# Third layer's edges of a graph network: cross product before the first map, destination rows gathered with adding transfers

## The reference, cut to what matters

```python
msg_s = (s_n @ Ws_src)[src] + (s_n @ Ws_dst)[dst]
msg_v = (v_n . Wv_src)[src] + (v_n . Wv_dst)[dst]
y0, y1 = rsh[:, 0], rsh[:, 1:4]
w1 = rbf @ W_rbf                                  # 16 -> 224 numbers an edge
m1_s, m1_v = cg_tp(msg_s, msg_v, y0, y1, *w1)
a = leaky_0.2(m1_s @ W_alpha); a = sum over 16 of (a * alpha_dot)     # 4 logits
val_s, val_v = m1_s @ Ws_val, m1_v . Wv_val
val_v = val_v * sigmoid(val_s @ Wg); val_s = sigmoid(val_s)
m2_s, m2_v = cg_tp(val_s, val_v, y0, y1, fixed weights)
h = m2_s @ Ws_vlin, m2_v . Wv_vlin

def cg_tp(s, v, y0, y1, w_ss, w_sv, w_vs, w_vv0, w_vv1):
    scalars = [w_ss * s * y0, w_vv0 * dot(v, y1) / sqrt(3)]
    vectors = [w_sv * s * y1, w_vs * v * y0, w_vv1 * cross(v, y1) / sqrt(2)]
```

## Time and profile before

| | us |
|---|---|
| median of 3 runs (lowest, highest) | 12669.28 (12666.13, 12681.18) |
| the profiled execution | 12702.04 |
| its span, first to last instruction | 12700.3 |
| mean granted TensorE clock | 0.791 of full speed |
| tables and their barrier | from 75.3 to about 166 |
| second layer's edge phase | from about 4188 to about 6750 |
| third layer's edge phase | from 7285.7 to about 9820 |

### The profile page before, as it was taken

One profiled execution on the slowest core, in us unless ns is written; L12 is line 12 of the kernel. 1 busy time (PEld: TensorE's weight loads), 2 busy tenths in 40 slices (PEclk: granted clock), 3 DMA queues, 4 the chain that ended last, 5 costly groups with the idle time before them and its releaser, 6 DMA issues. The chain is left out here.

```text
span 12700.3 us, 220425 instructions
## 1 busy us (share of the span) xinstructions
PE 9229.7 (73%) x44798; PEld 7244.6 (57%) x44798; DVE 8713.2 (69%) x21701; ACT 4529.6 (36%) x11637; POOL 8172.7 (64%) x8692
## 2 busy tenths in 40 slices
PE   2899999973655666666664578888887465999985
PEld 2888888863545322222223477777776454565654
DVE  4677777777643555555554389999999764667763
ACT  1455555540012222222221267777776001333331
POOL 4788888864843788888882176666664582666650
PEclk7777777776865777777776589999898786899995
...
GB/s 91 106 114 115 113 113 114 115 85 112 170 74 15 111 131 131 131 130 131 130 132 141 102 79 81 81 81 81 81 81 67 129 170 59 84 87 87 93 87 41
DMA packets 1339110, 1293.91 MB, mean 102 GB/s; under 512 B 504078, under 2 KB 1142018, under 8 KB 1338374
## 3 DMA queue, kind: packets, MB, share of 16 engines
...
...
## 5 line engine op out<-in xcount | busy, mean ns | idle before, releaser
L664 POOL DMA_INDIRECT e_gs<-tab_src,e_ix x1568 | 1708.1, 1089 | 763.2 <-issue 429.9
L664 POOL DMA_INDIRECT e_gd<-tab_dst,e_ix x1568 | 1610.7, 1027 | 477.8 <-issue 474.4
L715 PE MATMUL e_psS<-e_rows,e_same 128*128 128x480 f32 x1568 | 1113.6, 876 | 848.2 <-DVE e_same L689 848.2
L603 PE MATMUL e_psF<-w_ident,e_F 128*128 128x128 f32 x6272 | 1293.0, 315 | 246.9 <-ACT e_F L1822 233.0
L733 POOL DMA_INDIRECT acc<-e_sums,e_row x784 | 1247.5, 1591 | 239.0 <-issue 206.7
L715 PEld LDWEIGHTS e_psS<-e_rows,e_same 128*128 128x128 f32 x1568 | 430.6, 293 | 1541.7 <-issue 1514.7
L1642 POOL DMA_INDIRECT e_g<-tab_src,e_er x976 | 970.1, 994 | 525.1 <-issue 284.1
L633 ACT ACTIVATE e_FT<-e_psF 128x384 f32<-128x384 f32 (+1 forms) x2352 | 1078.0, 458 | 538.5 <-PE e_psF L603 526.4
L1431 PE MATMUL s_psS<-s_wv,s_hot 128*128 128x168 f32 (+1 forms) x3904 | 800.0, 361 | 615.2 <-POOL s_wv L1389 242.6
L603 PEld LDWEIGHTS e_psF<-w_ident,e_F 128*128 128x128 f32 x6272 | 895.5, 170 | 389.9 <-issue 346.0
L1431 PEld LDWEIGHTS s_psS<-s_wv,s_hot 128*128 128x128 f32 x3904 | 694.3, 228 | 720.4 <-issue 529.5
...
## 6 DMA issues: line engine op xcount, KB each, us to landing
s_val<-val SPq DMA_DIRECT2D x488, 320.0 KB
val<-e_O SPq DMA_DIRECT2D x392, 320.0 KB, 2.7
acc<-w_zeros SPq DMA_DIRECT2D x392, 139.5 KB
...
e_krow<-in_src_t SPq DMA_DIRECT2D x196, 256.0 KB
...
e_es<-in_es SPq DMA_DIRECT2D x196, 130.0 KB
e_gs<-tab_src,e_ix POOLq DMA_INDIRECT x1568
```

Of the source, the lines that this page charges most:

```text
L603: last = nc.tensor.transpose(psF[:, P * g:P * g + P], F[:, k, P * g:P * g + P], ident[:, :])
L664: pool.indirect_dma_start(into[t][u][:, k, :], None, tables[t], bass.IndirectOffsetOnAxis(ix[u][:, t, k:k + 1], 0))\
L715: nc.tensor.matmul(psS[(k) % len(psS)], T["same"][u][:, k, :], values[:, k, :], start=True, stop=True)\
```

## The change

Four things change, all for the third layer's edges.

1. **Adding transfers.** POOL gathers source rows into `msg` (four buffers), and one step later, when they have landed, gathers destination rows onto them with `compute_op=ALU.add` (line 1931 of the changed kernel). DVE's add of line 1945 and the buffers `gs` and `gd` are gone. POOL's wait for the reuse of a buffer is on `products` of the macro four before.
2. **Cross product first.** DVE makes all nine products of the message's vector with y1 (`nine`, 3 x 96 columns a tile), takes the dot product and the cross product from them, and multiplies the weights in. The map then gives only the part that goes with scalars as a third group of 32, so that after it two DVE instructions (2069, 2075) stand where eight stood. `O` is 292 wide, not 384.
3. **y0 through the weights.** `edge_tables` makes `es16_y0`, the 16 radial rows times y0, once: PE and ACT turn y0, SP stores it as `y0_t`, and then in eight rounds SP loads 8 pieces of `es16` and 8 of y0 (broadcast to 16 partitions), POOL multiplies 128 x 1568, and SP stores 8 pieces. In the edge phase the weight map takes 32 rows (16 plain, 16 scaled), SP loads one more piece a macro, and ACT's four scalings a macro of line 1822 (`e_msg_y`) are gone.
4. **Logits.** The part of the leaky unit that is linear is folded into the map (four columns, 160 to 163), so DVE has max and multiply in one instruction, a sum, and an add of 16 numbers. Setup has a few more small loads and DVE instructions on weights.

The diff, without unchanged lines:

```diff
@@ -394,12 +401,23 @@
+        Q, CH = ET // 7, EPAD // 8
+        PART = CH // 8
+        psY, y0T = S.ps("psY", [Q, 2, 512]), S.sb("y0T", [Q, 7, P])
+        es2, y2 = ([S.sb(f"{name}{u}", [P, PART]) for u in range(2)] for name in ("es2", "y2"))
+        def scaled_out(sp, n):
+            u = n % 2
+            sp.wait_ge(sem("scaled"), n + 1)
+            for c in range(8):
+                at = bass.ds(CH * c + PART * n, PART)
+                sp.dma_start(D["es16_y0"][:, at], es2[u][16 * c:16 * c + 16, :]).then_inc(sem(f"scaled_out{u}"), 16)
@@ -409,10 +427,30 @@
+            y0_row = D["y0_t"].rearrange("t p -> (t p)")
+            for n in range(8):
+                u = n % 2
+                if n > 1:
+                    sp.wait_ge(sem(f"scaled_out{u}"), 128 * (n // 2))
+                for c in range(8):
+                    at = bass.ds(CH * c + PART * n, PART)
+                    sp.dma_start(es2[u][16 * c:16 * c + 16, :], D["es16"][:, at]).then_inc(sem(f"scaled_in{u}"), 16)
+                if n == 0:
+                    sp.wait_ge(sem("y0_T"), 2)
+                    sp.dma_start(D["y0_t"].rearrange("(g q) p -> q g p", q=Q), y0T[:, :, :]).then_inc(sem("y0_out"), 16)
+                    sp.wait_ge(sem("y0_out"), 16)
+                for c in range(8):
+                    at = bass.ds(CH * c + PART * n, PART)
+                    sp.dma_start(y2[u][16 * c:16 * c + 16, :], y0_row[at].partition_broadcast(16)).then_inc(sem(f"scaled_in{u}"), 16)
+                if n:
+                    scaled_out(sp, n - 1)
+            scaled_out(sp, 7)
+            for u in range(2):
+                sp.wait_ge(sem(f"scaled_out{u}"), 128 * 4)
@@ -425,6 +463,10 @@
+            for n in range(8):
+                u = n % 2
+                pool.wait_ge(sem(f"scaled_in{u}"), 256 * (n // 2 + 1))
+                nc.gpsimd.tensor_tensor(es2[u][:, :], es2[u][:, :], y2[u][:, :], ALU.mult).then_inc(sem("scaled"), 1)
@@ -433,6 +475,10 @@
+            for n in range(2):
+                act.wait_ge(sem("y0_turned"), n + 1)
+                a, b = 4 * n, min(4 * n + 4, 7)
+                nc.scalar.activation(y0T[:, a:b, :], psY[:, n, 0:P * (b - a)].rearrange("q (g p) -> q g p", p=P), ACT.Copy).then_inc(sem("y0_T"), 1)
@@ -585,6 +645,49 @@
+X_A, X_D, X_C, X_X, X_B, X_W = 0, 64, 128, 224, 320, 384
+NINE_W, MSG_W = 384, CX + C1V
+def spread(ap, *dims):
+    return bass.AP(ap.tensor, ap.offset, [list(ap.ap[0]), *[list(d) for d in dims]])
+def dve_message_products(nc, dve, i, psW, msg, nine, dot, F, Y, S, free):
+    tt = nc.vector.tensor_tensor
+    v, crossed = msg[:, :, C0:CX], msg[:, :, CX:MSG_W]
+    tt(comp(nine[:, :, 0:3 * C1V]), bcast(v, 2, 3), bcast(Y, 3, C1V), ALU.mult).then_inc(S.sem("nine"), 1)
+    dve.wait_ge(S.sem("nine"), i + 1)
+    nc.vector.tensor_reduce(dot[:, :, :], nine[:, :, :].rearrange("p t (d c) -> p t c d", d=3)[:, :, 0:C1, :], AX.X, ALU.add)\
+        .then_inc(S.sem("dot"), 1)
+    tt(crossed[:, :, 0:C1], nine[:, :, 224:256], nine[:, :, 160:192], ALU.subtract)
+    tt(comp(crossed[:, :, C1:C1V], 2), comp(nine[:, :, 64:128], 2), comp(nine[:, :, 32:352], 2)[:, :, ::-1, 0:C1], ALU.subtract)\
+        .then_inc(S.sem("crossed"), 1)
+    dve.wait_ge(S.sem("weights"), i + 1)
+    wait(dve, *free)
+    tt(spread(F[:, :, X_A:], (X_W, TM), (X_B - X_A, 2), (1, C0)), comp(psW[:, :, 0:2 * C0], 2), bcast(msg[:, :, 0:C0], 2, 2), ALU.mult)
+    dve.wait_ge(S.sem("crossed"), i + 1)
+    tt(comp(F[:, :, X_C:X_C + C1V]), bcast(psW[:, :, 128:160], 2, 3), comp(v), ALU.mult)
+    tt(comp(F[:, :, X_X:X_X + C1V]), bcast(psW[:, :, 192:224], 2, 3), comp(crossed), ALU.mult)
+    dve.wait_ge(S.sem("dot"), i + 1)
+    tt(F[:, :, X_D:X_D + C1], psW[:, :, 160:192], dot[:, :, :], ALU.mult).then_inc(S.sem("products"), 1)
+def pe_message_maps(nc, pe, i, k, FT, o, W, w, rows, S, tag, ahead):
+    scalars = W[w + "_t0"].shape[1]
+    f = FT[:, k, :]
+    wait_apart(pe, S.sem(tag + "_FT"), i * TM + k + 1, S.sem("pe_passed"))
+    wait_apart(pe, S.sem(tag + "_O"), i * TM + k + 1 - ahead, S.sem("pe_passed"))
+    nc.tensor.matmul(o[:, 0:scalars], f[0:rows, 0:P], W[w + "_t0"][:, :], start=True, stop=True, skip_group_check=True)
+    nc.tensor.matmul(o[:, scalars:scalars + P], f[:, P:2 * P], W[w + "_t1"][:, :], start=True, stop=False, skip_group_check=True)
+    nc.tensor.matmul(o[:, scalars + C1:scalars + P], f[:, 2 * P:3 * P], W[w + "_t2"][:, :], start=False, stop=True,
+                     skip_group_check=True).then_inc(S.sem(tag + "_linear"), 1)
@@ -1789,11 +1893,16 @@
+                if m := i_of_ring(0):
+                    i, u, j = m
+                    wait_apart(sp, sem(f"msg{u}"), j * 16 * TM, sem("sp_passed"))
+                    for n, k in enumerate(("src", "dst")):
+                        sp.dma_start(ix[u][:, n, :], D[k][:, bass.ds(i * TM, TM)]).then_inc(sem(f"ix{u}"), 16)
-                    sp_indices(sp, i, u, j, ix, D, ("src", "dst"), S, [sem("gathered0"), sem("gathered1")])
-                    sp.dma_start(es[u][:, :], D["es16"][:, bass.ds(i * ME, ME)]).then_inc(sem(f"es{u}"), 16)
+                    sp.dma_start(es[u][0:16, :], D["es16"][:, bass.ds(i * ME, ME)]).then_inc(sem(f"es{u}"), 16)
+                    sp.dma_start(es[u][16:32, :], D["es16_y0"][:, bass.ds(i * ME, ME)]).then_inc(sem(f"es{u}"), 16)
@@ -1805,11 +1914,22 @@
+            passed = sem("pool_passed")
-                i_of = by_two(i_of_ring)
-                if m := i_of(0):
-                    pool_gather(nc, pool, *m, ix, (D["tab_src"], D["tab_dst"]), (gs, gd), S, (sem("msg"), m[0] - 1))
+                if m := i_of_ring(0):
+                    i, u, j = m
+                    wait_apart(pool, sem(f"ix{u}"), (j + 1) * 32, passed)
+                    wait_apart(pool, sem("products"), i - RING + 1, passed)
+                    for k in range(TM):
+                        pool.indirect_dma_start(msg[u][:, k, 0:CX], None, D["tab_src"], bass.IndirectOffsetOnAxis(ix[u][:, 0, k:k + 1], 0))\
+                            .then_inc(sem(f"from_src{u}"), 16)
+                if m := i_of_ring(ADD):
+                    i, u, j = m
+                    wait_apart(pool, sem(f"from_src{u}"), (j + 1) * 16 * TM, passed)
+                    for k in range(TM):
+                        pool.indirect_dma_start(msg[u][:, k, 0:CX], None, D["tab_dst"], bass.IndirectOffsetOnAxis(ix[u][:, 1, k:k + 1], 0),
+                                                compute_op=ALU.add).then_inc(sem(f"msg{u}"), 16)
@@ -1858,13 +1978,6 @@
-                if m := i_of(JOIN):
-                    i, u, j = m
-                    act.wait_ge(sem("msg"), i + 1)
-                    wait(act, sem("products"), i)
-                    for k in range(TM):
-                        last = times_y0(msg0, msg, i, k)
-                    last.then_inc(sem("msg_y0"), 1)
@@ -1876,9 +1989,9 @@
-                    if m := i_of(JOIN):
+                    if m := i_of(WEIGHTS):
-                        wait_apart(pe, sem(f"es{u}"), (j + 1) * 16, passed)
+                        wait_apart(pe, sem(f"es{u}"), (j + 1) * 32, passed)
@@ -1918,17 +2031,16 @@
-                nc.vector.memset(f[:, :, 352:F_W], 0.0).then_inc(sem("padded"), 1)
+                nc.vector.memset(f[:, :, 96:128], 0.0).then_inc(sem("padded"), 1)
-                    wait(dve, sem("dot"), i)
-                    wait(dve, sem("products2"), i - SECOND_IN + PRODUCT)
-                    dve_products(nc, dve, i, psW, msg, msg0, prod, dot, F[u], Y(i)(0, 3), S,
-                                 (sem("msg"), i + 1), (sem("lin_turned"), (i - 1) * TM), (sem("msg_y0"), i + 1))
+                    _, v, turn = i_of_ring(PRODUCT)
+                    dve.wait_ge(sem(f"msg{v}"), (turn + 1) * 16 * TM)
+                    dve_message_products(nc, dve, i, psW, msg[v], nine, dot, F[u], Y3(i), S, (sem("lin_turned"), (i - 1) * TM))
@@ -1936,33 +2048,31 @@
-                    tt(V2, comp(O[i_of_ring(SECOND_IN)[1]][:, :, 160:256]), bcast(F2[u][:, :, F2_W:F2_W + C1], 2, 3), ALU.mult).then_inc(sem("gated"), 1)
-                if m := i_of(JOIN):
-                    i, u, j = m
-                    dve.wait_ge(sem(f"gathered{u}"), (j + 1) * 16 * 2 * TM)
-                    wait(dve, sem("products"), i)
-                    wait(dve, sem("msg_y0"), i)
-                    tt(msg[:, :, :], gs[u][:, :, :], gd[u][:, :, :], ALU.add).then_inc(sem("msg"), 1)
+                    tt(V2, comp(O[i_of_ring(SECOND_IN)[1]][:, :, VEC:VEC + C1V]), bcast(F2[u][:, :, F2_W:F2_W + C1], 2, 3), ALU.mult).then_inc(sem("gated"), 1)
-                    nc.vector.scalar_tensor_tensor(out=lk[:, :, :], in0=a, scalar=0.2, in1=a, op0=ALU.mult, op1=ALU.max)\
-                        .then_inc(sem("leaky"), 1)
+                    nc.vector.scalar_tensor_tensor(out=lk[:, :, :], in0=a, scalar=0.0, in1=bcast(W["l2_adot"][:, :], 1, TM), op0=ALU.max,
+                                                   op1=ALU.mult).then_inc(sem("leaky"), 1)
```

(39 more changed lines are left out.)

31 lines of the change are left out of this document (20 added, 11 removed).

## The result

The changed kernel takes 13,042.6 us (median of 4 runs, 13,033.16 to 13,055.8) against 12,667.7 (4 runs, 12,645.73 to 12,681.18) of the kernel before beside it: 1.0295 times, 95% interval 1.0280 to 1.0309, so 375 us slower. Forecast were 12,845 us and a range up to 12,970: the side was right, the size was not. The profiled execution took 13,042.75 us, its span 13,041.0.

The account below looks back on a forecast made before the run. The prediction took DVE to bound the third layer's edge phase and POOL to take over at 13.05 us a macro. 12702 + 91 (edges) + 85 (tables) + 2 (setup) = 12880, less 33, gave 12,845 us; range 12,580 to 12,970.

Parts of the forecast that it names:

- What bounds it, and that POOL takes over: Third layer's edge phase: DVE sets the pace before, at 12.59 us a macro; after the change POOL does, at 13.05.
- DVE's part, 10.7 us: Third layer's edge phase: DVE's need a macro falls from 12.59 us by 7.15 removed and 5.25 added.
- An adding transfer costs 1.59 whatever its row: POOL's adding transfers: 1.59 us each, as in the second layer, the split read as the adding's, not the row size's.
- Nine packets an engine: Second layer's adding transfers: 143 packets each, nine an engine, one for each of eight rows and one more.
- I take 13.05: POOL's time a macro in the third layer's edge phase, from the second layer's 13.1 and 12.98 us: +90 us.
- Bounds of the edge phase: Adding transfer's cost: 1.02 us at least, 1.59, or something above if an add into SBUF costs more than into memory.
- The tables: +85 forecast: Tables phase: SP's new chain of loads and stores ends it at 251 us against 166; bounds +55 to +120.
- Start and end of the phase, +1: Third layer's edge phase: +10 us before the first product, -9 us after the last.
- Waits put at nothing: Edge phase: POOL's waits for source rows and for `products` cost nothing; PE's 32-row weights stream as many columns.
- Rivals 1 and 2: Adding transfer costs 1.3 us, 12,650 us in all, chance 0.16; or the same as a gather, 12,463, chance 0.17.
- rival 3: PE's clock falls to 0.65 in the edge phase, which takes 370 us more instead of 90: 13,125 us, chance 0.09.
- Sum: Whole kernel: profiled 12702 us + 91 edge phase + 85 tables + 2 setup = 12880, less 33: about 12,845.

Follow-up runs that it names:

- all_one: Changed kernel with every third-layer edge-phase DVE instruction having two SBUF inputs given one input: 12,753.0 us, 1.0071 of the kernel before.
- cross_one: Changed kernel with the second cross product's eight DVE instructions given one input instead of two: 12,887.2 us, 1.0171 of the kernel before.
- adds_alone: Kernel before with the adding transfers alone: 12,804.0 us, 1.0100 of the kernel before; on another chip 13,876.6 us, 0.9602.

## Why the prediction was wrong in size, point by point

- **What bounds it, and that POOL takes over: right.** POOL has only issue as idle time, DVE waits for the adds' rows before each of 195 products.
- **DVE's part, 10.7 us: right within 0.4 us.** 14.05 less 3.74 of idle time is 10.3.
- **An adding transfer costs 1.59 whatever its row: right for the transfer by itself.** Rows of 640 bytes took 1.55 in all_one, rows of 1920 bytes 1.57 at the median. Nine packets an engine, argued from the earlier trace rows, came as well: 136050 packets of the software queue in 7500 to 10000, less 48 for each of 711 gathers, over some 708 adds, is 144.
- **"I take 13.05": this step failed.** I carried the second layer's pace over to the third. The bare transfers need 4 x 1.85 + 4 x 1.27 = 12.5 us (all_one: 12.45), and the second layer's 13.05 stands 0.6 us over that. I put this 0.6 down to DVE, busy 57% there; no run tests that layer. In the third layer the lengthening is 14.05 - 12.45 = 1.6 us, of which the second cross product alone makes 0.93 (cross_one). The missing 1.0 us, times 195, is 195 us, and 13,042.6 less the forecast 12,845 is 198. The traces before had the sign of it: gathers of 0.94 us at least, but 1.138 and 1.021 in the mean, and I put that down to nothing.
- **Bounds of the edge phase: the upper one had no number.** "Something above if an add into SBUF costs more" named the wrong reason and gave no price.
- **The tables: +85 forecast, +87.2 measured** at their end (89.6 less 2.4 by which setup ended later), though y0's store took longer than I gave it (14 us, waiting behind the wide loads) and a round less (14.2 to 14.8 us from the third on, against 15.2). That it would all reach the end is not borne out: without the chain the time is 47 us less, and why is open.
- **Start and end of the phase, +1: +3.** Start 19.2 us against 12.4, end 55 against 59.
- **Waits put at nothing** (source rows, the reuse of buffers, PE's map of 32 rows): none shows.
- **Rivals.** Rivals 1 and 2, a cheaper add, fell by all_one. In rival 3 PE's clock fell to 0.86 only, with PE behind POOL.
- **Sum.** 195 x 1.455 + 3 = 287 for the edge phase and 89.6 for setup and tables: 376, against a difference of medians of 375. That it meets so closely is partly luck: the two profiled executions differ by 341, and the other phases differ by up to some 20 us each, of both signs.

The Trainium skill's page "SBUF — State Buffer" (section "Who interferes with whom") says that a DVE instruction with two SBUF inputs contends with a GpSimd instruction that reads SBUF, and that tensor_reduce never contends. By these two sentences cross_one and all_one come out as measured, if POOL reads SBUF while it writes an indirect transfer's descriptors; no run here shows what it reads. The same section takes `tensor_copy` for what stalls descriptor writing, and tensor_tensor for what does not; here it was the other way, 0.05 us for copies against 0.93 for tensor_tensor on the third add.

What stays open: which moment of a transfer is held, and why one cross product costs 1.0 us beside one add, while with two of them a macro in adds_alone each add is only 0.1 to 0.2 us longer in the mean (0.5 at most); and the loops that give back part of the chain's time.
